# A fused mixer-and-experts block: its table of steps laid out with later landing times for two images

## The chip, the cores and the metric

The kernel runs on one core of one Trainium2 chip. The metric is the device time of one execution in microseconds (us); a change of about 1% is what a measurement of it can tell.

## What is computed

The input is 16 images of 64 channels by 16 x 16 pixels. Each image goes through a mixer with a depthwise convolution and a linear-attention product, and then each of its 256 tokens through a gated mixture of eight experts, of which two have weight:

```
x = x + conv_block(_ln_c(x))         # normalised over channels
  zxbcdt = x @ W_in.T                # z, (x, B, C), dt
  xBC = silu(depthwise 3x3 conv(xBC) + conv_b);  dt = softplus(dt + dt_bias)
  KV = einsum(B, xs * dA);  y = einsum(C, KV) + xs * D
  y = layernorm(y * silu(z)) * ln_g + ln_b;  out = y @ W_out.T
t = t + ffn(_ln_t(t))                # t: the tokens of x
  probs = softmax(xf @ gate_w + gate_b); cw = the top two of probs, else 0
  for e in 8 experts:  out += cw[:, e] * (gelu(xf @ W1[e] + b1[e]) @ W2[e] + b2[e])
```

## The kernel before

The 16 images are four groups of four (g = 0 to 3). A group is one pass of about 110 steps; a step has a short name and the group's number behind it, so `sq2` is the step "square the image" of group 2, the third. (Names such as `sq20` are the step `sq2` of group 0: the square behind the mixer. `x20` is likewise the step `x2` of group 0.) Groups share two sets of buffers by `g % 2`.

One list of tokens, `PLAN`, written out by hand as a table of text, sets the order of everything. Every engine walks the same list (`walk`) and emits the steps that have code in its own function, so each engine runs its steps strictly in the order of the list, and between engines only semaphores order the work. A step that waits therefore holds back all that stands behind it on its engine, and nothing on the others but what needs them.

The steps that matter here:

- Head of the kernel: `tb`, `tap` (VectorE) and `tw`, `tT` (TensorE) fold the depthwise taps into weight matrices; ScalarE's `tf` and VectorE's `te` copy them from PSUM to `wT`. `wa`, `wb` centre the experts' weights (`wae`, `wbe` copy them back). `busy` is a matmul on junk.
- Normalising group g: `sq` (ScalarE, L478) squares the image, `sm` (TensorE, L978) sums it, `se` copies the sums, `tr` transposes them, `ve` (VectorE) makes the variance, `pw` (GpSimd, L384) the reciprocal root, `rx` (ScalarE, L558) widens it, `rb` (TensorE, L991) transposes it back, `xn` (VectorE, L787) multiplies.
- Mixer: `cv0`, `cv1`, `cv2` (L1014, six matmuls a step, which the trace counts as twelve), `xs`, `z`, `sz`, `bd`, `bcp`, `k0` to `k2`, `bcs` (B and C's own convolution on VectorE), `dtv`, `ex`, `sf0`, `sf1` (softplus), `xt`, `v`, `bt`, `btc`, `kv`, `kvc`, `y`, `y0`, `y1`; then `gs`, `ps` (L1075), `stc`, `stt`, `gst`, `pwg`, `rxg`, `rbg`, `pj`, `pc`, `x2` for the second normalisation and the projection. `c0` and `cf` make a constant of the projection, `nm`, `nT` and `ne` prepare its weights.
- Experts: `sq2`, `s2`, `s2e`, `t2`, `ve2`, `pw2`, `rx2`, `rb2`, `xn2` normalise the tokens; `rt0`, `th`, `rt1`, `rt2` route them; `cwt` (L1107), `cwc` and the DMA step `gw` spread the eight weights to `gates` by way of DRAM. Expert e is `u` (up, L1124), `h` (gelu on ScalarE, L585), `d` (down, L1137), `m` (weigh on VectorE, L909), `a` (add on GpSimd, L419), each with the expert's number. Group 3 has PSUM banks of its own for this (its "lane"), the others share one set.

The image loads are not in `PLAN`. SyncE issues them ahead of it, those of groups 2 and 3 as the last of all:

```
            sp.dma_start(w2[:], W2.rearrange("e f c -> f e c")).then_inc(d_exp, 16)
            load(2)
            load(3)
```

ScalarE's square waits for its image by itself (`act.wait_ge(d_x[g], 32)`). Before a step whose function needs another table, ScalarE runs a one-element instruction, which loads the table (L440); the places follow from the order.

Of the kernel before, what the change touches and what calls it, by code (L numbers as in the profile page):

```python
# [15 lines left out]


PLAN = """
busy0 busy0 busy0 busy0 busy0 busy0 busy0 busy0 sq0 busy0 tb0 tw0 tap0 busy0 ta0 busy0 busy0 sm0 busy0 se0 busy0
tr0 tT0 ve0 ini0 sq1 sq2 pw0 wa0 te0 tf0 busy0 dtv0 rx0 sm1 wae0 rb0 wb0 se1 xn0 ex0 sf00 tr1 wbe0 cv00 sq3 ea0  # L20
ve1 nm0 pw1 bd0 cv10 bcp0 sf10 rx1 k00 cv20 k10 k20 nT0 xs00 rb1 xs10 z0 xn1 bcs0 xt00 dtv1 sz00 bd1 v00 sz10
xt10 ne0 bcp1 bt0 cv01 k01 v10 ex1 btc0 k11 kv0 cv11 kvc0 k21 sf01 bcs1 y0 sm2 cv21 se2 y00 gs00 y10 tr2 xs01
c00 ve2 gs10 xs11 sf11 ps0 pw2 cf0 xt01 stc0 stt0 z1 gst0 rx2 dtv2 rb2 pwg0 sz01 pj0 xn2 sz11 v01 xt11 rxg0 bd2
v11 pc0 rbg0 bcp2 bt1 x20 cv02 btc1 k02 sq20 s20 k12 kv1 s2e0 t20 cv12 ve20 ex2 kvc1 pw20 k22 y1 rx20 rt00 cv22
y01 th0 rb20 rt10 xs02 xs12 z2 xn20 gs01 rt20 u00 bcs2 sz02 y11 cwt0 xt02 cwc0 sz12 gw0 xt12 sf02 gs11 pj1 bt2
ps1 sf12 h00 pc1 u10 v02 stc1 btc2 stt1 v12 h10 d00 gst1 kv2 pwg1 u20 kvc2 y2 m00 rxg1 sm3 h20 y02 a00 d10 se3
rbg1 m10 gs02 tr3 u30 ve3 d20 x21 h30 pw3 u40 y12 sq21 a10 rx3 s21 rb3 m20 s2e1 gs12 t21 xn3 d30 a20 h40 ve21
bd3 dtv3 pw21 cv03 m30 bcp3 ex3 a30 rx21 rt01 rb21 cv13 k03 th1 xn21 rt11 u50 cv23 h50 k13 rt21 d40 xs03 k23
cwt1 xs13 z3 cwc1 ps2 gw1 m40 bcs3 sf03 a40 xt03 stc2 sz03 stt2 u60 sz13 xt13 gst2 d50 sf13 pwg2 pj2 h60 bt3 m50
rxg2 u70 v03 a50 btc3 pc2 rbg2 v13 x22 kv3 d60 kvc3 sq22 m60 y3 h70 s22 y03 s2e2 t22 u01 ve22 d70 y13 pw22 h01  # L30
gs03 u11 m70 a60 gs13 rt02 d01 h11 a70 pj3 m01 th2 u21 rx22 st0 rt12 a01 rb22 h21 d11 xn22 pc3 u31 rt22 m11 cwt2
cwc2 h31 ps3 gw2 a11 d21 stc3 stt3 u41 gst3 m21 pwg3 h41 d31 a21 u51 rxg3 m31 rbg3 h51 a31 d41 x23 u61 m41 sq23
h61 s23 a41 d51 s2e3 t23 m51 u71 ve23 d61 h71 pw23 m61 u02 a51 rx23 rt03 d71 h02 rb23 a61 m71 th3 u12 xn23 a71
rt13 u03 h12 st1 d02 h03 rt23 u22 m02 cwt3 u13 cwc3 h22 gw3 a02 d12 h13 u32 m12 d03 a12 h32 d22 u42 m22 u23 a22
h42 d32 h23 u52 m32 u33 a32 h52 m03 d42 a03 d13 m42 u62 a42 h33 m13 d23 a13 h62 u43 m23 d52 a23 h43 d33 m52 u53
a52 m33 d43 h53 a33 d62 m43 u63 a43 m62 d53 h63 u72 m53 u73 a53 h72 d63 a62 h73 d72 m63 a63 d73 m72 m73 a72 a73
st2 st3
""".split()


# [1128 lines left out]
```

## Time and profile before

| | us |
|---|---|
| median of 3 runs (lowest, highest) | 181.52 (181.01, 182.63) |
| the profiled execution | 181.16 |
| its span, first to last instruction | 179.3 |

| engine | busy us | share of span |
|---|---|---|
| TensorE (PE) | 152.0 | 85% |
| VectorE (DVE) | 121.2 | 68% |
| ScalarE (ACT) | 95.0 | 53% |
| GpSimd (POOL) | 64.5 | 36% |

The profile is of one execution. PE is TensorE's matmuls, PEld its weight loads, which overlap them. An idle time in brackets is followed by what ended it. The granted clock is 1.00 at TensorE's full speed.

### The profile page before, as it was taken

The numbers are of one execution on the slowest core, as the hardware profiler recorded it, in microseconds if no ns is written. First come the engines' busy times: TensorE is split into PE (matmuls) and PEld (weight loads), VectorE is DVE, ScalarE is ACT, GpSimd is POOL, SyncE is SP. The second block draws the span as 40 slices with busy tenths as digits, with TensorE's granted clock in tenths as the row PEclk, the third lists the DMA queues.
The fourth block names the chain that finished last, engine by engine and source line by source line (L and its number), as shares of the span: only waits on it lengthen the run. The fifth ranks groups of instructions, "written<-read, shape, count | busy, mean of one in ns | idle before, by whom it ended". The sixth has DMA issues, their size and how long they took to land.

```text
span 179.3 us, 2932 instructions
## 1 busy us (share of the span) xinstructions
PE 152.0 (85%) x966; PEld 61.2 (34%) x966; DVE 121.2 (68%) x330; ACT 95.0 (53%) x182; POOL 64.5 (36%) x83
## 2 busy tenths in 40 slices
PE   6930499999899999798899997895889699999960
PEld 2410334445444545343343443232232222223210
DVE  1640087899779899769999988995446973353461
ACT  1600524591662678746857674673474655855430
POOL 7430012000060300146530260652655623588580
PEclk9995589999999999999999999999999999999997
DMA  4604200000000000891000199020693025950004
GB/s 107 165 15 96 83 4 0 0 2 0 4 2 0 4 0 7 212 225 37 0 0 0 35 238 207 5 60 7 175 216 79 0 62 139 218 119 0 4 0 117
DMA packets 8344, 11.84 MB, mean 66 GB/s; under 512 B 3842, under 2 KB 7306, under 8 KB 7306
## 3 DMA queue, kind: packets, MB, share of 16 engines
q1 hardware_dynamic: 7152, 11.05, 26.9%
q10 hardware_dynamic: 1178, 0.61, 1.3%
q8 instruction: 8, 0.13, 0.3%
q14 instruction: 6, 0.05, 0.1%
HBM read 10.48 MB, written 1.18 MB: 65 GB/s over the span
## 4 chain that ended last, share of the span: by engine, by line
PE 63%; DVE 15%; issue 8%; DMA 5%; POOL 3%; ACT 3%; SPq 0%; DVEq 0%; POOLq 0%; ACTq 0%
PE pm L1014 14%; PE pe L1137 7%; PE pe L1124 6%; PE pe L1014 5%; PE pm L1137 4%; PE pm L1124 4%; DMA gates<-cwd 4%; PE pr L1141 3%; DVE tmp L909 3%; PE pm L1024 2%; PE pr L1075 2%; POOL acc L419 1%; DVE lg L671 1%; PE pm L1032 1%; PE pm L991 1%
## 5 line engine op out<-in xcount | busy, mean ns | idle before, releaser
L419 POOL TENSOR_TENSOR acc<-acc,tmp 128x512 f32<-128x512 f32 x27 | 34.3, 1276 | 26.1 <-DVE tmp L909 25.6
L585 ACT ACTIVATE hid<-pe,b1T 128x512 f32<-128x512 f32 x48 | 30.2, 681 | 12.5 <-PE pe L1124 12.3
L1124 PE MATMUL pe<-fst,w 64*128 64x512 f32 x96 | 26.9, 635 | 2.3 <-ACT hid L585 2.3
L909 DVE SCALAR_TENSOR_TENSOR tmp<-pe,b2T,gates 128x512 f32<-128x512 f32 x24 | 17.9, 746 | 13.9 <-PE pe L1137 12.6
L1137 PE MATMUL pe<-hid,w 128*64 128x512 f32 x96 | 25.8, 613 | 1.5 <-DVE tmp L909 1.5
L1014 PE MATMUL pm<-pad,wT 64*128 64x512 f32 x108 | 25.1, 600 | 0.0
L384 POOL TENSOR_TENSOR r<-ve,halves 128x8 f32<-128x8 f32 x4 | 6.6, 1662 | 40.9 <-DVE dtp L624 21.1
L612 DVE SCALAR_TENSOR_TENSOR bcc<-bcp,cw_bc,bcc 128x256 f32<-128x256 f32 x32 | 15.4, 482 | 1.0
L585 ACT ACTIVATE hid<-pm,b1T 128x512 f32<-128x512 f32 x16 | 10.1, 686 | 6.8 <-PE pm L1124 5.3
L1014 PEld LDWEIGHTS pm<-pad,wT 64*128 64x128 f32 x108 | 9.9, 185 | 11.0 <-issue 11.0
L402 POOL TENSOR_TENSOR rg<-ge,halves 128x8 f32<-128x8 f32 x4 | 6.6, 1642 | 18.5 <-DVE ge L863 18.5
L1124 PEld LDWEIGHTS pe<-fst,w 64*128 64x128 f32 x96 | 7.5, 184 | 15.4 <-issue 14.7
L409 POOL TENSOR_TENSOR r<-ve,halves 128x8 f32<-128x8 f32 x4 | 6.6, 1644 | 16.5 <-DVE ve L890 16.5
L440 ACT ACT_TABLE_LOAD x9 | 11.5, 1283 | 0.2
L909 DVE SCALAR_TENSOR_TENSOR tmp<-pm,b2T,gates 128x512 f32<-128x512 f32 x8 | 6.0, 750 | 7.4 <-PE pm L1137 6.7
L1124 PE MATMUL pm<-fst,w 64*128 64x512 f32 x32 | 8.7, 622 | 1.4 <-DVE fst L896 1.4
L1137 PEld LDWEIGHTS pe<-hid,w 128*64 128x64 f32 x96 | 5.1, 135 | 13.9 <-issue 9.5
L787 DVE TENSOR_TENSOR pad<-xin,pm 128x512 f32<-128x512 f32 x3 | 2.0, 683 | 10.9 <-PE pm L991 10.9
L978 PE MATMUL pe<-xin,sums 128*32 128x128 f32 x8 | 0.7, 417 | 9.7 <-issue 9.7
L1137 PE MATMUL pm<-hid,w 128*64 128x512 f32 x32 | 8.5, 609 | 0.2 <-DVE tmp L909 0.2
L1014 PE MATMUL pe<-pad,wT 64*128 64x512 f32 x36 | 8.5, 606 | 0.0
L478 ACT ACTIVATE sq<-xin 128x512 f32<-128x512 f32 x4 | 2.5, 624 | 10.5 <-DMA xin<-in_x_dram 10.4
(221 smaller groups left out, 249.6 us busy)
## 6 DMA issues: line engine op xcount, KB each, us to landing
gates<-cwd SPq DMA_DIRECT2D x16, 512.0 KB, 7.3
xin<-in_x_dram SPq DMA_DIRECT2D x7, 128.0 KB, 2.9
out_dram<-acc SPq DMA_DIRECT2D x7, 128.0 KB, 2.8
w<-in_L_ffn_W_dram SPq DMA_DIRECT2D x2, 256.0 KB, 3.4
w<-in_L_ffn_W_dram ACTq DMA_DIRECT2D x1, 256.0 KB, 4.4
xin<-in_x_dram ACTq DMA_DIRECT2D x1, 128.0 KB, 2.7
cwd<-cwS SPq DMA_DIRECT2D x4, 32.0 KB
out_dram<-acc ACTq DMA_DIRECT2D x1, 128.0 KB, 2.5
```

The source lines that it names most:

```text
L384: pool.tensor_tensor(r1[p][:], ve[p][:], halves[:], ALU.pow).then_inc(rstd.sem, 1)
L402: pool.tensor_tensor(rg[p][:], ge[p][:].rearrange("p j q -> p (j q)"), halves[:], ALU.pow).then_inc(o_rstd.sem, 1)
L409: pool.tensor_tensor(r2[p][:], ve2[p][:], halves[:], ALU.pow).then_inc(rstd2.sem, 1)
L419: pool.tensor_tensor(acc[p][:], (x2 if e == 0 else acc)[p][:], tmp[ln][e % 2][:], ALU.add).then_inc(summed[ln].sem, 1)
L440: act.activation(scrap[:, n:n + 1], zero[:], FUNCTION[step])
L585: act.activation(hid[ln][e % 2][:, q, :], expert_banks(g)[q][:], ACT.Gelu, bias=b1T[:, e:e + 1]).then_inc(hid_in[ln].sem, 1)
L612: dve.scalar_tensor_tensor(out=bcc[p][:], in0=view, scalar=cw_bc[:, t:t + 1], in1=bcc[p][:], op0=ALU.mult, op1=ALU.add).then_inc(bc_conv.s ...
L909: dve.scalar_tensor_tensor(out=tmp[ln][e % 2][:], in0=expert_banks(g)[2][:], scalar=b2T[:, e:e + 1], in1=gates[p][:, e, :], op0=ALU.add, o ...
L1014: ins = pe.matmul((b0, b1)[q][:], wT[half, t, :], pad[p][half, :, t // 3:t // 3 + HH, t % 3:t % 3 + WW], start=(t == 0), stop=(t == TAPS - 1))
L1124: ins = pe.matmul(expert_banks(g)[q][:], w1[half, e, :], fst[p][half, :], start=True, stop=True)
L1137: ins = pe.matmul(expert_banks(g)[2][C * q:C * q + C, :], w2[:, e, :], hid[ln][e % 2][:, q, :], start=True, stop=True)
L1141: pe.matmul(pr[1][:], junk[:, 0:P], junk[:], start=True, stop=True)
```

## The change

The table `PLAN` is written anew; no instruction's code is touched. All steps of before are in it, and one more `busy` (463 tokens for 461). The order on SyncE is the same; on the other four engines it is another. The head of the table:

```diff
-busy0 busy0 busy0 busy0 busy0 busy0 busy0 busy0 sq0 busy0 tb0 tw0 tap0 busy0 ta0 busy0 busy0 sm0 busy0 se0 busy0
-tr0 tT0 ve0 ini0 sq1 sq2 pw0 wa0 te0 tf0 busy0 dtv0 rx0 sm1 wae0 rb0 wb0 se1 xn0 ex0 sf00 tr1 wbe0 cv00 sq3 ea0
...
+busy0 busy0 busy0 busy0 busy0 busy0 busy0 busy0 sq0 busy0 tb0 busy0 tw0 tap0 busy0 ta0 busy0 busy0 sm0 busy0 se0
+busy0 tr0 tT0 ini0 ve0 pw0 wa0 tf0 te0 sq1 busy0 rx0 dtv0 sm1 rb0 ex0 se1 wb0 xn0 ea0 wae0 sf00 tr1 cv00 wbe0
...
```

ScalarE's order in the kernel's head, before; `sq0<-xin2` is the square of the third group's image, `sq1<-xin3` that of the fourth, `wT<-pe1` is `tf0`, `r1w0` is `rx0`:

```order
L478 ACTIVATE sq1<-xin1 128x512
L478 ACTIVATE sq0<-xin2 128x512
L452 ACTIVATE wT<-pe1 128x512
L558 ACTIVATE r1w0<-r10 128x512
L457 ACTIVATE w1<-pm2 128x512
L483 ACTIVATE s11<-pe0 128x256
L488 ACTIVATE dtu0<-dta0 128x64
L457 ACTIVATE w1<-pr0 128x512
L478 ACTIVATE sq1<-xin3 128x512
L461 ACTIVATE expA<-alog 128x8
```

The same place in the changed kernel:

```order
L452 ACTIVATE wT<-pe1 128x512
L478 ACTIVATE sq1<-xin1 128x512
L558 ACTIVATE r1w0<-r10 128x512
L488 ACTIVATE dtu0<-dta0 128x64
L483 ACTIVATE s11<-pe0 128x256
L461 ACTIVATE expA<-alog 128x8
L457 ACTIVATE w1<-pm2 128x512
L457 ACTIVATE w1<-pr0 128x512
```

The two squares are gone from here. They stand 14 to 15 rows further on, behind `btc0` (`bT0<-pm0`):

```order
L466 ACTIVATE woT<-pr0 128x64 x2
L467 ACTIVATE b1T<-pr0 128x8
L468 ACTIVATE b2T<-pr0 128x8
L515 ACTIVATE bT0<-pm0 128x8x16
L478 ACTIVATE sq0<-xin2 128x512
L478 ACTIVATE sq1<-xin3 128x512
L523 ACTIVATE gsq0<-g0 128x512
```

On TensorE, the stretch from the end of the first group's convolution (`xs0`, `bc0`, `v0` are group 0's) to the second group's first third (`pad1`), before:

```order
L991 MATMUL pe1<-ident,r1w1 128x128 x4
L1024 MATMUL pm2<-pad0,wT 128x512
L1024 MATMUL pm0<-pad0,wT 128x512
L1032 MATMUL pm1<-ident,xs0 128x128 x4
L1001 MATMUL pe2<-pad1,wbc 32x256 x4
L1032 MATMUL pm2<-ident,xs0 128x128 x4
L1038 MATMUL pm0<-ident,bc0 128x128 x2
```

and after:

```order
L991 MATMUL pe1<-ident,r1w1 128x128 x4
L1141 MATMUL pr1<-junk 128x512
L1024 MATMUL pm2<-pad0,wT 128x512
L1024 MATMUL pm0<-pad0,wT 128x512
L1032 MATMUL pm1<-ident,xs0 128x128 x4
L953 MATMUL pr0<-ident,wgc 128x64
L954 MATMUL pr0<-ident,wo_raw 128x64
L955 MATMUL pr0<-ident,b1_raw 128x8
L956 MATMUL pr0<-ident,b2_raw 128x8
L1032 MATMUL pm2<-ident,xs0 128x128 x4
L1038 MATMUL pm0<-ident,bc0 128x128 x2
L1001 MATMUL pe2<-pad1,wbc 32x256 x4
L1045 MATMUL pm0<-v0,bT0 32x128 x8
```

The projection's weights (`ident,wgc` and the three rows behind) now stand between the two transposes of `xs0`, the junk matmul is the added one, and `kv0` (`v0,bT0`) comes before the second group's convolution and not behind its first third.

Late in the kernel, on TensorE, around the first expert of group 3 (`pm0<-fst1,w1`) and the transpose `cwt3` (`ident,cw1`); `fst0` is group 2's input, before:

```order
L1102 MATMUL pr1<-ident,r2w1 128x128 x4
L1124 MATMUL pe0<-fst0,w1 128x512
L1124 MATMUL pe1<-fst0,w1 128x512
L1124 MATMUL pm0<-fst1,w1 128x512
L1124 MATMUL pm1<-fst1,w1 128x512
L1137 MATMUL pe2<-hid00,w2 64x512 x2
L1124 MATMUL pe0<-fst0,w1 128x512
L1124 MATMUL pe1<-fst0,w1 128x512
L1107 MATMUL pr1<-ident,cw1 64x128
```

and after:

```order
L1102 MATMUL pr1<-ident,r2w1 128x128 x4
L1124 MATMUL pe0<-fst0,w1 128x512
L1124 MATMUL pe1<-fst0,w1 128x512
L1137 MATMUL pe2<-hid01,w2 64x512 x2
L1124 MATMUL pm0<-fst1,w1 128x512
L1124 MATMUL pm1<-fst1,w1 128x512
L1124 MATMUL pe0<-fst0,w1 128x512
L1124 MATMUL pe1<-fst0,w1 128x512
L1107 MATMUL pr1<-ident,cw1 64x128
```

Group 3's first expert now stands behind one more down pass of group 2, and an up pass of group 2 and `cwt3` stand right behind it. In between these places, from the fourth group's mixer on, expert passes `u5` and `u6` of group 1 stand ahead of `cv03`, `bd3` behind it, `h6` behind `th1`, `kvc3` behind `rt02`, `xn22` behind `y03`, and `ps3`, `stt3` and `pj3` behind `cwt2` and `u51`.

## Rows read from the trace of the kernel before

**Rows 1.** The page, parts 1 and 5.
```profile
PE 152.0 (85%) x966; PEld 61.2 (34%) x966; DVE 121.2 (68%) x330; ACT 95.0 (53%) x182; POOL 64.5 (36%) x83
...
L585 ACT ACTIVATE hid<-pe,b1T 128x512 f32<-128x512 f32 x48 | 30.2, 681 | 12.5 <-PE pe L1124 12.3
...
L440 ACT ACT_TABLE_LOAD x9 | 11.5, 1283 | 0.2
```

**Rows 2.** Chain of waits in order of time: start us, us, what.
```profile
9.59 0.86 PE pm L947 x2
...
10.67 9.71 issue
20.38 1.08 PE pe L978 x16
21.46 1.05 PE pm L991 x4
22.50 1.56 PE pr L947 x2
...
24.28 2.78 PE pm L1014 x12
...
33.31 0.59 PE pe L991 x4
...
43.99 0.57 PE pm L978 x16
```

**Rows 3.** Timeline of ScalarE: start us, us, instruction [idle before, releaser].
```profile
8.15 0.63 ACT L478 ACTIVATE sq<-xin 128x512 f32<-128x512 f32 x1
19.16 0.63 ACT L478 ACTIVATE sq<-xin 128x512 f32<-128x512 f32 x1 [10.38 <-DMA xin<-in_x_dram]
...
20.18 0.62 ACT L558 ACTIVATE r1w<-r 128x512 f32<-128x512 f32 x1
```

**Rows 4.** Timelines of GpSimd and of VectorE, the first group's head.
```profile
9.53 1.66 POOL L384 TENSOR_TENSOR r<-ve,halves 128x8 f32<-128x8 f32 x1 [2.67 <-DVE ve L778]
...
22.64 0.69 DVE L787 TENSOR_TENSOR pad<-xin,pm 128x512 f32<-128x512 f32 x1 [10.60 <-PE pm L991]
```

**Rows 5.** Windows: us, then busy time of each engine, granted clock, DMA.
```profile
12.00:13.00 1.00, 0.00 (x0) 0.00 (x0) 0.04 (x1) 0.00 (x0) 0.00 (x0) 1.00 0.16 27
13.00:14.00 1.00, 0.00 (x0) 0.00 (x0) 0.00 (x0) 0.00 (x0) 0.00 (x0) 0.77 0.04 0
...
120.00:124.00 4.00, 2.02 (x17) 0.60 (x17) 3.46 (x14) 1.23 (x4) 0.74 (x2) 1.00 0.12 29
```

**Rows 6.** Timeline of SyncE, which issues the loads.
```profile
13.00 0.30 SPq L314 DMA_DIRECT2D b_raw<-in_L_ffn_b_dram  x1
...
15.56 2.58 SPq L294 DMA_DIRECT2D xin<-in_x_dram  x4
```

**Rows 7.** Timeline of TensorE, the second group's statistics.
```profile
48.63 0.65 PE L1075 MATMUL pr<-g,onesd 128*32 128x128 f32 x16 [0.56 <-ACT gsq L523]
```

**Rows 8.** What TensorE waited for, 78 to 174: total us, times, longest.
```profile
PE pr L1107 <- DVE cw L723: 1.7, 2, 1.5
...
PE pm L1124 <- DVE fst L896: 1.4, 1, 1.4
```

**Rows 9.** The window from 78 to 174, columns as in rows 5.
```profile
78.00:174.00 96.00, 87.22 (x501) 29.91 (x499) 67.85 (x167) 57.24 (x102) 48.41 (x37) 1.00 0.36 81
```

**Rows 10.** Timeline of VectorE: routing's first step, first and second group.
```profile
62.15 0.23 DVE L671 TENSOR_TENSOR lg<-t,r 128x64 f32<-128x64 f32 x1
...
90.04 1.28 DVE L671 TENSOR_TENSOR lg<-t,r 128x64 f32<-128x64 f32 x1
```

**Rows 11.** Timelines of ScalarE and VectorE: the fourth group's gates, a lone pass.
```profile
146.73 0.27 ACT L553 ACTIVATE cwS<-pr 64x128 f32<-64x128 f32 x1 [1.37 <-PE pr L1107]
...
156.02 0.75 DVE L909 SCALAR_TENSOR_TENSOR tmp<-pm,b2T,gates 128x512 f32<-128x512 f32 x1 [0.60 <-DMA gates<-cwd]
...
171.40 0.75 DVE L909 SCALAR_TENSOR_TENSOR tmp<-pm,b2T,gates 128x512 f32<-128x512 f32 x1 [2.17 <-PE pm L1137]
```

More of the change, by code:

```diff
@@ L18 @@
 PLAN = """
-busy0 busy0 busy0 busy0 busy0 busy0 busy0 busy0 sq0 busy0 tb0 tw0 tap0 busy0 ta0 busy0 busy0 sm0 busy0 se0 busy0
-tr0 tT0 ve0 ini0 sq1 sq2 pw0 wa0 te0 tf0 busy0 dtv0 rx0 sm1 wae0 rb0 wb0 se1 xn0 ex0 sf00 tr1 wbe0 cv00 sq3 ea0
-ve1 nm0 pw1 bd0 cv10 bcp0 sf10 rx1 k00 cv20 k10 k20 nT0 xs00 rb1 xs10 z0 xn1 bcs0 xt00 dtv1 sz00 bd1 v00 sz10
-xt10 ne0 bcp1 bt0 cv01 k01 v10 ex1 btc0 k11 kv0 cv11 kvc0 k21 sf01 bcs1 y0 sm2 cv21 se2 y00 gs00 y10 tr2 xs01
-c00 ve2 gs10 xs11 sf11 ps0 pw2 cf0 xt01 stc0 stt0 z1 gst0 rx2 dtv2 rb2 pwg0 sz01 pj0 xn2 sz11 v01 xt11 rxg0 bd2
@@ L24 @@
[L24 to L37, printed above, removed]
+busy0 busy0 busy0 busy0 busy0 busy0 busy0 busy0 sq0 busy0 tb0 busy0 tw0 tap0 busy0 ta0 busy0 busy0 sm0 busy0 se0
+busy0 tr0 tT0 ini0 ve0 pw0 wa0 tf0 te0 sq1 busy0 rx0 dtv0 sm1 rb0 ex0 se1 wb0 xn0 ea0 wae0 sf00 tr1 cv00 wbe0
@@ new lines @@
+ve1 sf10 pw1 bd0 cv10 bcp0 rx1 dtv1 k00 ex1 cv20 k10 k20 rb1 xs00 busy0 xs10 z0 nm0 bcs0 xt00 sz00 xn1 nT0 sz10
+v00 xt10 ne0 bt0 v10 bd1 btc0 sq2 kv0 bcp1 sf01 sq3 cv01 kvc0 k01 y0 sm2 y00 cv11 k11 gs00 se2 y10 tr2 cv21 ve2
+gs10 sf11 pw2 ps0 xs01 k21 xs11 z1 stc0 rx2 stt0 xt01 gst0 sz01 c00 rb2 v01 sz11 pwg0 xt11 cf0 xn2 bcs1 pj0 v11
+rxg0 bd2 dtv2 pc0 rbg0 bcp2 bt1 x20 cv02 btc1 k02 sq20 s20 k12 kv1 s2e0 t20 cv12 ve20 ex2 kvc1 pw20 k22 y1 rx20
+rt00 cv22 y01 th0 rt10 rb20 xs02 bcs2 z2 xn20 xs12 rt20 u00 sz02 sz12 y11 cwt0 bt2 cwc0 xt02 gs01 gw0 xt12 sf02
@@ new lines @@
+gs11 ps1 pj1 sf12 h00 btc2 u10 stc1 v02 v12 stt1 h10 d00 gst1 kv2 pc1 pwg1 u20 kvc2 y2 h20 m00 sm3 y02 a00 rxg1
+d10 rbg1 gs02 m10 u30 se3 x21 a10 tr3 h30 d20 ve3 sq21 u40 m20 pw3 y12 s21 h40 d30 a20 s2e1 dtv3 u50 rx3 m30 t21
+h50 rb3 ve21 d40 xn3 pw21 u60 m40 cv03 a30 rx21 rt01 gs12 a40 th1 h60 rt11 rb21 d50 xn21 pj2 rt21 ex3 u70 m50
+cwt1 bd3 cwc1 ps2 gw1 a50 bcp3 k03 d60 stc2 stt2 cv13 gst2 h70 k13 pwg2 pc2 m60 u01 rxg2 k23 a60 rbg2 h01 cv23
+sf03 bcs3 x22 d70 xs03 z3 m70 sq22 xs13 sf13 s22 a70 xt03 s2e2 sz03 t22 st0 d01 ve22 sz13 bt3 v03 pw22 xt13 btc3
@@ new lines @@
+m01 u11 v13 a01 rt02 h11 kv3 u21 kvc3 th2 rt12 d11 h21 y3 m11 rx22 u31 rt22 a11 rb22 h31 y03 d21 u41 xn22 gs03
+m21 cwt2 h41 y13 d31 a21 cwc2 gw2 u51 m31 gs13 ps3 a31 stc3 h51 stt3 pj3 gst3 d41 pwg3 pc3 u61 m41 rxg3 a41 h61
+rbg3 d51 x23 u71 m51 sq23 h71 s23 a51 d61 s2e3 t23 m61 u02 ve23 d71 h02 pw23 m71 u12 a61 rt03 rx23 d02 h12 rb23
+a71 m02 th3 u22 xn23 a02 st1 rt13 d12 h22 u03 rt23 u32 h03 m12 cwt3 cwc3 d03 h32 gw3 a12 d22 u13 m22 u42 a22 h13
+d32 h42 u23 m32 u52 a32 h23 d42 h52 u33 m42 u62 a42 m03 d13 a03 d52 h33 m13 a13 d23 h62 u43 m23 m52 u72 a23 h43
@@ L38 @@
+d33 a52 h72 u53 m33 a33 d62 h53 d43 m62 u63 a62 m43 d53 h63 a43 m53 u73 a53 d63 h73 d72 m63 d73 a63 m72 m73 a72
+a73 st2 st3
 """.split()
```

## The prediction

> **What bounds the kernel now.** I read the page first, then the chain of waits, then each engine's timeline around the holes of the chain. TensorE is busy 152.0 us, 85% of the span [rows 1]. The chain of waits runs along TensorE nearly everywhere, so the time is TensorE's work plus its holes plus the two ends. One hole dwarfs the others: 9.71 us from 10.67 to 20.38, put down to "issue" [rows 2]. What it really is stands in ScalarE's timeline: the square of the second group's image ends at 8.78, and the next instruction in ScalarE's order is the square of the third group's image, which waits 10.38 us for its transfer and starts at 19.16 [rows 3]. Behind it in the same queue stand `tf0`, the copy of the taps' transpose, and `rx0`, which widens the first group's reciprocal root into r1w and ran at 20.18 [rows 3]; TensorE needs them for `sm1` and `rb0`. The transfer was only issued at 15.56 or later, behind all small loads, the last of which were issued at 13.00 and after [rows 6]. So ScalarE waits in line for data that nobody needs yet. After the hole the order is dense: of the 96 us from 78 to 174 TensorE is busy 87.22 [rows 9], and waits are short [rows 8].
>
> **The change, part 1: sq2 and sq3 leave ScalarE's head.** They stand now behind `btc0`. The work is the same, so what counts is when the convolution of the first group (`cv00`) starts; it started at 24.28 [rows 2]. I walk the new head. The transposes of `tT` end as before, at 9.59, `wa0` at 10.45 and the filler at 10.67 [rows 2]. ScalarE does `tf0` as soon as the transposes are out (to about 9.95), then sq1 to about 10.55 (0.63 us [rows 3]). `sm1` then takes 0.57 us at full clock, as `sm2` does, against 1.08 in the hole's wake [rows 2]: 10.67 to 11.25. `rb0` needs `rx0`, which needs GpSimd's power, 9.53 plus 1.66, so 11.19 [rows 4], plus 0.62 for the widening [rows 3] and some 0.2 of hand-over: 12.05. It takes 0.59 instead of 1.05, `wb0` 0.86, as its twin `wa0` did at 9.59, instead of 1.56 [rows 2], and the two transposes of `tr1` 0.22. That gives 12.05 + 0.59 + 0.86 + 0.22 = 13.7 for `cv00`. Its input, `xn0`, is ready at 12.65 + 0.1 + 0.69 = 13.4 [rows 4], so it isn't late. Gain at this point: 24.28 - 13.72 = 10.55 us, of which 9.71 is the hole less a new one of 0.8, and 1.7 the half clock.
>
> What is late next? The biases' loads were issued before 13.0 [rows 6]. The convolution of B and C, their first user, follows `cv00` by some 5 us, so at about 18.7, and `nm0`, which reads the loads of 13.0 and was moved behind that convolution, comes at about 23.3. The third image had landed at 19.16 [rows 3]; the squares of the third and fourth are now due at 26.3. All have several us in hand, so I cost those waits at nothing; were the cover gone, each us late would be a us on the path.
>
> **Part 2: the new order up to 67 us.** `ex1` goes ahead of `xs00`, so two table loads go from ScalarE, beside which TensorE was working anyway: nothing. `kvc0` now stands behind the seven small steps of `sf01` on VectorE, but TensorE has `cv01` meanwhile, a third of a convolution, which takes 2.8 us as that of 24.28 did [rows 2]: nothing. `cv11` moves behind `sm2` and `c0` behind `ps0`, so that TensorE no longer waits 0.56 us for the square of g at 48.63 [rows 7]: gain 0.55. From `x20` to `th0` the two orders are the same, so the lead is 11.1 us and stays so; `u10` waits for `h00` in both. I place the end of `y2` at 66.9 (before 78.0). One junk matmul more (0.22 us) fills a stretch in which TensorE waits for `xs00` anyway.
>
> **Part 3: the rest, 78 to 174 us in the profile.** TensorE's holes are 96 - 87.22 = 8.8, less 0.6 after its last matmul, so 8.2 us [rows 9]. The largest are 1.5 before `cwt2`, which waits for the routing's last step on VectorE, and 1.4 before the fourth group's first expert (`u03`), which waits for `xn23` [rows 8]. In the new order `xn22` stands behind `y03`, and `cwt2` waits for it too; but `ps3` has been taken out from behind `cwt2`. `u03` stands later, behind `u22` and `d12`, when `xn23` is done: that 1.4 goes. Walked step by step with the durations of the trace, the new order's holes are about 0.35 before `d10`, 0.3 before `tr3`, 0.4 in small ones up to `kv3`, 0.7 before `u21`, 0.85 before `cwt2`, 0.45 before `d31`, and nine from 0.1 to 0.45 in the last 45 us, among them one for the fourth group's gates (0.45); sum about 6.3. The hole before `u21` shows how: ScalarE copies `btc3` until 100.4; `h11` then needs a table load (1.28) and its warm-up instruction (0.2), then two activations at 0.681 each less their overlap, 1.25 in all [rows 1], so it ends at 103.1, while TensorE's last step before, `kv3`, ended at 102.5; hand-over 0.1. That before `cwt2`: VectorE ends `rt22` at 108.4, `y03` and `xn22` (1.5 and 0.7) follow, so 110.65; TensorE ended `u41` at 109.8. Gain 1.9. Bounds: from both sides, no hole at all would gain 8.2; a rearrangement as poor as the worst stretch of before (120 to 124 us, where TensorE works 2.02 of 4 us [rows 5]), met twice more, would lose 2 to 4. I take 1.9, since short waits on neighbours are what the trace shows everywhere. What follows the last matmul (the last weighing, the last addition, the stores) is the same in both.
>
> My walk takes VectorE's small steps mostly at their lone price. The trace shows the dear one: the first of the routing takes 0.23 us alone and 1.28 us beside a GpSimd addition [rows 10]. The Trainium skill (page "SBUF — State Buffer", section "SBUF: two separate sides") has the rule: VectorE with two SBUF inputs and GpSimd lock one shared pair of ports for a whole instruction. The trace agrees with it. By that rule a denser schedule has more such meetings; at 1.05 us each by the rows, and about every second one on the path, two more would make 1 us. I leave it in the range.
>
> **Sum.** 10.55 + 0.55 + 1.9 = 13.0 us. The profiled execution took 181.16 us (span 179.3 and 1.86 around it), so 168.2; it lies 0.36 below the median of the runs, 181.52, so I forecast **168.5 us**.
>
> **The rivals.**
>
> *The later order gives some back* (chance 0.15). The experts' passes are pulled ahead (`u50`, `u60` before `cv03`), while `h60` waits behind `th1`, this behind `rt01`, this behind GpSimd's power `pw21` (1.65 us) and the power behind addition `a20`. If this chain and the one through `xn22` each cost 1.5 to 2 us instead of what I walked, the holes are 10 and not 6.3: 172 us. For it: part 3 of the order is new nearly throughout; against it: TensorE has three convolution steps of 2.8 us each to lay over these waits.
>
> *The clock falls in the new head as well* (0.07). The granted clock was still at full (2.4 GHz) in 12 to 13 us and fell to half (1.2 GHz) in the next us; TensorE had stood still since 10.67 [rows 2, 5]. It stayed full over waits of 1.5 us (120 to 124) [rows 5]. In the new head TensorE stands still for 0.8 us only, at 11.25 to 12.05. If it fell all the same, `sm1`, `rb0` and `wb0` would cost their 1.7 us again and the first convolution 1 to 2 more: 171 to 172 us. The Trainium skill (page "TensorE: Matmul & The Clock Gate", section "Part 4: PE-mode transpose") says that transposes don't count as busy the way matmuls do, and much of the head is transposes; by that rule this rival is the outcome. No row bears it out: the head's first transposes end at 9.59 [rows 2], and the clock was full in 12 to 13 [rows 5].
>
> *The later order fills nearly all holes* (0.1): at 2 to 4 us left, 164.5 to 166.5.
>
> *The hole isn't what I take it for* (0.04): a wait for several things is put down to the last, and another small load could be as late as the image. Then the gain is 0 to 8 us: 173 to 181. Against it: what stood behind the square ran without a further wait [rows 3].
>
> *Slower* (0.02). The fourth group's gates reach VectorE by DMA; from the copy at 146.73 to the first weighing at 156.02 it takes 9.3 us, ended by the DMA [rows 11]. They now land at about 143 us, while the third group still has passes that share TensorE with the fourth's. A pass that stands alone lasts 0.75 + 2.17 = 2.9 us from weighing to weighing [rows 11]. If the gates came only when the third group was done, at about 157, all eight passes of the fourth would stand alone: 8 x 2.9 = 23 us behind 157, then the end of 6, so a span of 186 and 188 us in all. It makes the kernel slower from about 7 us later than I place them.
>
> **Chances and range.** The forecast (166.5 to 170) has 0.62; the others as given. The range from 165.5 to 172.5 leaves out the end of the fullest order, the false hole and the slow case, about 0.15 in all. A measurement of this kernel tells about 1% from no change: faster by more than that (below 179.7) has 0.96, no change 0.02, slower 0.02.
>
> **What would show it.** In the changed kernel's profile ScalarE's third square should start at about 26 us without a DMA wait; `cv00` should start near 13.7 with the granted clock at full throughout; `y2` should end near 67; TensorE's holes from there to its last matmul (near 160) should add up to 6 or 7 us, with the largest before `cwt2` and `u21`; the span should be near 166. I am wrong if a new wait on a small load opens before 25 us, if the clock halves, or if the holes behind 67 us add up to 10 or more.

## The result, and the profile after

| | before | changed |
|---|---|---|
| median of 4 runs each, us | 181.86 | 173.53 |
| lowest to highest, us | 181.01 to 182.63 | 173.15 to 175.08 |
| profiled execution (its span), us | 181.16 (179.3) | 173.71 (171.8) |

The ratio is 0.9559, with a 95% interval of 0.9485 to 0.9634: the change makes the kernel 4.4% faster. I had forecast 168.5 us, with a range up to 172.5. The gain is 8 us where I had summed 13.

The page of the changed kernel, its busy times, granted clock and the chain's shares:

```profile
PE 151.1 (88%) x968; PEld 60.9 (35%) x968; DVE 123.9 (72%) x330; ACT 92.1 (54%) x178; POOL 64.9 (38%) x83
...
PEclk9999999999999999999999999999999999999995
...
PE 42%; DVE 28%; DMA 10%; issue 7%; POOL 6%; ACT 4%; SPq 1%; DVEq 0%; POOLq 0%; ACTq 0%
```

The chain's shares before:

```profile
PE 63%; DVE 15%; issue 8%; DMA 5%; POOL 3%; ACT 3%; SPq 0%; DVEq 0%; POOLq 0%; ACTq 0%
```

VectorE has done the same 330 instructions as before, in 2.7 us more [rows 1], and its share of the chain has nearly doubled. That is the first sign of what went wrong.

The head, on the chain of waits (start, length, what). It answers to [rows 2]:

```profile
9.75 0.18 DVE ve L778
...
10.01 1.67 POOL r L384
...
11.69 0.64 ACT r1w L558
...
12.37 0.66 PE pm L991 x4
13.03 0.86 PE pr L947 x2
13.89 0.22 PE pe L986 x2
14.11 2.78 PE pm L1014 x12
```

ScalarE's timeline (start, length, line, operation, in brackets the idle time before it), to be held against [rows 3]:

```profile
9.88 0.60 ACT L452 ACTIVATE wT<-pe 128x512 f32<-128x512 f32 x1 [1.40 <-PE pe L936]
10.37 0.62 ACT L478 ACTIVATE sq<-xin 128x512 f32<-128x512 f32 x1
11.69 0.63 ACT L558 ACTIVATE r1w<-r 128x512 f32<-128x512 f32 x1 [0.70 <-POOL r L384]
...
27.01 1.14 ACT L478 ACTIVATE sq<-xin 128x512 f32<-128x512 f32 x2
```

The 10 us hole is gone. The third image's square runs at 27.01 without a wait, and the convolution of the first group starts at 14.1 in place of 24.3. The clock is full up to the last of the 40 slices, which lies behind the last matmul.

The rest, by windows of the span (us, busy time and instructions of PE, PEld, DVE, ACT, POOL, clock), from the end of `y2` to the last matmul; it answers to [rows 9]:

```profile
68.20:166.00 97.80, 87.00 (x501) 30.34 (x499) 70.19 (x166) 57.24 (x102) 48.25 (x36) 1.00 0.36 79
```

TensorE's holes there are 97.80 - 87.00 = 10.8 us. They were 8.2 before, and I had walked 6.3. TensorE's waits, from 68 to 166 us, against [rows 8]:

```profile
PE pe L1137 <- DVE tmp L909: 2.1, 3, 0.9
PE pr L1107 <- DVE cw L723: 1.7, 2, 0.9
PE pr L1107 <- DVE fst L896: 1.3, 1, 1.3
PE pr L1091 <- ACT sq L538: 1.0, 2, 0.5
PE pe L1124 <- ACT hid L585: 0.8, 2, 0.4
PE pm L1137 <- DVE tmp L909: 0.8, 2, 0.6
PE pm L1045 <- DVE v L823: 0.7, 1, 0.7
```

Five of these seven rows, 6.6 us, end on VectorE. The longest, before `cwt2`, was 0.85 us in my walk and is 1.3. VectorE's and GpSimd's timelines ahead of it show why:

```profile
105.58 1.29 DVE L671 TENSOR_TENSOR lg<-t,r 128x64 f32<-128x64 f32 x1
...
111.01 1.04 DVE L717 TENSOR_TENSOR o<-k,kk 128x64 f32<-128x64 f32 x1
```
```profile
105.51 1.27 POOL L419 TENSOR_TENSOR acc<-x,tmp 128x512 f32<-128x512 f32 x1
110.66 1.31 POOL L419 TENSOR_TENSOR acc<-acc,tmp 128x512 f32<-128x512 f32 x1 [3.87 <-DVE tmp L909]
```

Two small steps that take 0.22 us alone take 1.29 and 1.04 here, and `xn22`, which `cwt2` waits for, stands behind both. Each ends 0.08 to 0.09 us after the addition that ran beside it: 105.58 + 1.29 = 106.87 against 105.51 + 1.27 = 106.78, and 112.05 against 111.97. They were held until the addition was over. In the order of before `L717` met none: 225 ns in the mean of its four, by the same grouping of before as the following rows. The groups of VectorE in the changed kernel by line (busy us, mean ns, idle time ahead):

```profile
L874 DVE SCALAR_TENSOR_TENSOR x<-xo,c,xin 128x512 f32<-128x512 f32 x4 | 3.5, 881 | 0.3
L795 DVE TENSOR_TENSOR dtv<-t,r 128x64 f32<-128x64 f32 x4 | 2.0, 490 | 0.9 <-POOL r L384 0.9
L717 DVE TENSOR_TENSOR o<-k,kk 128x64 f32<-128x64 f32 x4 | 1.7, 430 | 0.1
```

Before, their means were 752, 222 and 225 ns. Each has one step of four that met an addition and grew. A step with a single input, `L689` (`TENSOR_SCALAR td<-th`), was held too: at 136.12 it took 0.89 us, where it takes 0.18 alone, and ended at 137.01, behind an addition that ran to 136.95.

One correction to my text ahead of the result: the table has two junk matmuls more, not one (463 tokens against 461). One stands ahead of `tw0`, in the kernel's head; the other ahead of `z0`.

### The profile page after: what moved, and what is told of

Read it like the earlier page. It is cut to its first block, busy times and chain, and to the rows that moved or that the text cites. A ratio compares the mean times of both kernels' runs of the same rounds, so it can differ in the third digit from the quotient of the medians.

```text
span 171.8 us, 2932 instructions
## 1 busy us (share of the span) xinstructions
PE 151.1 (88%) x968; PEld 60.9 (35%) x968; DVE 123.9 (72%) x330; ACT 92.1 (54%) x178; POOL 64.9 (38%) x83
## 4 chain that ended last, share of the span: by engine, by line
PE 42%; DVE 28%; DMA 10%; issue 7%; POOL 6%; ACT 4%; SPq 1%; DVEq 0%; POOLq 0%; ACTq 0%
PE pm L1014 9%; DMA gates<-cwd 7%; PE pe L1014 5%; PE pr L1141 4%; PE pm L1137 4%; DVE tmp L909 3%; PE pm L1124 3%; DVE bcc L612 2%; DMA cwd<-cwS 2%; PE pe L1137 2%; DVE lg L671 2%; POOL r L409 2%; POOL r L384 2%; DVE g L849 1%; PE pm L1024 1%
## 5 line engine op out<-in xcount | busy, mean ns | idle before, releaser
L1124 PE MATMUL pe<-fst,w 64*128 64x512 f32 x96 | 26.3, 623 | 1.5 <-ACT hid L585 1.5
L612 DVE SCALAR_TENSOR_TENSOR bcc<-bcp,cw_bc,bcc 128x256 f32<-128x256 f32 x32 | 16.4, 511 | 1.0
L1014 PEld LDWEIGHTS pm<-pad,wT 64*128 64x128 f32 x108 | 9.9, 186 | 10.7 <-issue 10.2
L1124 PEld LDWEIGHTS pe<-fst,w 64*128 64x128 f32 x96 | 8.0, 185 | 14.1 <-issue 13.5
L523 ACT ACTIVATE gsq<-g 128x512 f32<-128x512 f32 x8 | 5.0, 626 | 12.8 <-DVE g L849 12.7
L1141 PE MATMUL pr<-junk 128*128 128x512 bf16 x17 | 7.2, 565 | 1.5 <-DVE zero L593 1.5
L849 DVE TENSOR_TENSOR g<-g,sz 128x512 f32<-128x512 f32 x8 | 6.6, 822 | 0.3
```

Source lines behind the costliest of these rows:

```text
L612: dve.scalar_tensor_tensor(out=bcc[p][:], in0=view, scalar=cw_bc[:, t:t + 1], in1=bcc[p][:], op0=ALU.mult, op1=ALU.add).then_inc(bc_conv.s ...
L849: dve.tensor_tensor(g_[p][:, q, :], g_[p][:, q, :], sz[p][:, q, :], ALU.mult).then_inc(g_dve.sem, 1)
L1014: ins = pe.matmul((b0, b1)[q][:], wT[half, t, :], pad[p][half, :, t // 3:t // 3 + HH, t % 3:t % 3 + WW], start=(t == 0), stop=(t == TAPS - 1))
L1124: ins = pe.matmul(expert_banks(g)[q][:], w1[half, e, :], fst[p][half, :], start=True, stop=True)
L1141: pe.matmul(pr[1][:], junk[:, 0:P], junk[:], start=True, stop=True)
```

## The experiments

Kernels are named by what they are; ratios are to the kernel before, run on the same chip. Differences between two of the kernels are those of their medians of four to six runs with a spread of 1 to 2 us, and some pairs ran on different chips, so a few tenths in them mean nothing. The head's start adds to this: in seven profiled executions that share the changed kernel's head, `cv00` starts anywhere from 12.81 to 14.04 us. Where a difference in the rest of the kernel matters, I therefore also give it from the end of `y2` on, from the profiled executions.

### Which part of the order costs: new head with the old rest, and the reverse

The table is cut right behind `y2` of group 2. The first kernel has the changed table up to there and before's behind it; against the changed table:

```diff
 ... kv2 pc1 pwg1 u20 kvc2 y2
-h20 m00 sm3 y02 a00 rxg1 d10 rbg1 gs02 m10 u30 se3
+m00 rxg1 sm3 h20 y02 a00 d10 se3 rbg1 m10 gs02 tr3
...
```

> The changed kernel's table up to step h20 (the end of y2 on TensorE), then the table of before. In the changed kernel TensorE reaches the end of y2 at 68.2 us, 9.9 us ahead of before, but its last matmul only 7.4 us ahead. Theory A, the new order of the later part is itself worse by 2.5 us: this kernel keeps the whole lead of 9.9 us, TensorE's holes behind y2 add up to 8.2 us as in before, span near 169.4 and time near 171.2 us. Theory B, whatever order follows loses the lead (later meetings of VectorE and GpSimd, or the gates' transfers, fall otherwise): the time is that of the changed kernel, 173.5 us.

Measured: 171.60 us (170.68 to 172.33), ratio 0.9423 (0.9336 to 0.9509). The second is the reverse cut: before's table up to `y2`, the changed one behind it.

> The table of before up to the same place, then the changed kernel's. Theory A: the hole on ScalarE's third square is back and the later part loses its 2.5 us as well, so slower than before by 2.5 us, near 184 us. Theory B: the later part of the new order is as good as the old one here, 181.5 us.

Measured: 186.01 us (184.70 to 186.15), ratio 1.0201 (1.0126 to 1.0276). The new rest makes the kernel slower with either head: by about 1.9 us on the new one (173.53 against 171.60; from the end of `y2` to the last matmul the profiled executions take 97.7 and 95.8) and by 4.2 on the old, where I had expected 2.5 (the spans of the profiled executions are 4.8 apart, 184.1 against 179.3). Of these 4.8, 3.1 lie in the rest: from the start of `z2` to that of the last matmul it takes 108.86 us where before takes 105.80. The others lie in the head, where the granted clock stayed at half longer than in before, which had it full from 24 to 28 us. The windows of the second kernel:

```profile
20.00:24.00 4.00, 3.00 (x22) 2.13 (x23) 0.74 (x2) 2.43 (x6) 0.00 (x0) 0.50 0.01 3
24.00:28.00 4.00, 4.00 (x13) 1.57 (x14) 3.17 (x14) 1.21 (x3) 1.18 (x1) 0.63 0.02 4
```

TensorE's waits from 60 us on in the first kernel (new head, old rest), the third and fourth row:

```profile
...
PE pr L1107 <- DVE cw L723: 1.7, 2, 1.5
PE pm L1124 <- DVE fst L896: 1.4, 1, 1.4
```

The wait for `xn23` of 1.4 is back, and yet the sum of the holes is 8.6 (96.00 - 87.40, from 67.9 to 163.9), 2.2 less than with the new rest.

### Is the hole what I took it for: the squares alone, and the loads alone

Before with only two tokens moved:

```diff
-... ini0 sq1 sq2 pw0 ... cv00 sq3 ea0 ...
+... ini0 sq1 pw0 ... cv00 ea0 ...
...
-... ex1 btc0 k11 ...
+... ex1 btc0 sq2 sq3 k11 ...
```

> The table of before with two tokens moved: sq2 and sq3 stand behind btc0, as in the changed kernel; nothing else. If the wait of the third square was the whole gain, cv00 starts near 13.5 us (one junk matmul less ahead of it than in the changed kernel), y2 ends at or before 68 us, and the time is 170.5 to 171.5 us by theory A and 173 us by theory B. If the rest of the new head order was needed (ex1 early, nm0 late behind the loads of 13 us), a new wait of VectorE on the loads in nm0 opens near 16 us and the time is 172 to 175 us.

Measured: 171.43 us (170.43 to 172.00), ratio 0.9411 (0.9339 to 0.9482). Two tokens give the whole of the change's gain, and 2 us more. `cv00` starts at 12.87. The new wait that the expectation named did open: VectorE waits 1.17 us for the biases' load in `nm0`, until 16.64, and TensorE has the convolution meanwhile.

The counter-test leaves the table of before as it is and only issues the third and fourth images' loads earlier:

```diff
             load(1)
+            load(2)
+            load(3)
             sp.dma_start(dtb[:], rows(dt_bias, P)).then_inc(d_dt, 16)
...
             sp.dma_start(w2[:], W2.rearrange("e f c -> f e c")).then_inc(d_exp, 16)
-            load(2)
-            load(3)
```

> The kernel before with its table of steps untouched: only the loads of the third and fourth images are issued right behind the second's, ahead of the small loads. If ScalarE's wait for the third image is the whole hole, sq2 can run at 11 to 12 us, a little late for tf0 and rx0, and cv00 starts at 14.5 to 16: a gain of 8 to 10 us, 172 to 174. If the hole was another, small load's, it is now issued some 2 us later and the time is 181 to 184. A new wait is possible at the small loads, for the biases ahead of the convolution of B and C (due near 19) or for A_log (13): up to 2 us more.

Measured: 171.57 us (171.14 to 172.76), ratio 0.9432 (0.9352 to 0.9512). The third square, still in its old place in ScalarE's order, waits 0.30 us in place of 10.38:

```profile
9.09 0.63 ACT L478 ACTIVATE sq<-xin 128x512 f32<-128x512 f32 x1 [0.30 <-DMA xin<-in_x_dram]
9.63 0.58 ACT L452 ACTIVATE wT<-pe 128x512 f32<-128x512 f32 x1
```

`cv00` starts at 13.67. One small load comes late, the biases' for `nm0` on VectorE:

```profile
17.69 0.28 DVE L757 TENSOR_TENSOR wg<-wo_raw,lng 64x128 f32<-64x128 f32 x1 [1.42 <-DMA b_raw<-in_L_ffn_b_dram]
```

It costs TensorE little: from the start of `cv00` to the end of `y2` this execution takes 54.5 us, and before 54.0. So the wait for the image was the whole hole, and there were two ways to remove it, neither of which needs a new rest. My expectation (172 to 174) had the square push `tf0` further back than it did: the image lands 2 us sooner than I had assumed.

### The added junk matmuls

```diff
-busy0 tb0 busy0 tw0 tap0
+busy0 tb0 tw0 tap0
...
-busy0 xs10 z0 nm0
+xs10 z0 nm0
```

> The changed kernel without the two junk matmuls that its table has more than before (the one ahead of tw0 and the one ahead of z0). By the traces the first moves tw0 from 5.41 to 5.83 us and so the whole head by 0.42; the second fills a wait. So 0.4 us less than the changed kernel, about 173.1 us. The rival: the head is bound by VectorE's tap products and not by the junk, then no difference.

Measured: 173.19 us (173.15 to 173.67), ratio 0.9519 (0.9458 to 0.9581). That is 0.34 less, as expected. In its profiled execution `cv00` starts at 12.82, 1.2 us sooner than in the changed kernel's (14.04 in the same view), but this can't be put down to the junk: the kernel with one fill for each addition, below, has both junk matmuls and the changed head, and its `cv00` starts as early:

```profile
12.81 2.85 PE L1017 MATMUL pm<-pad,wT 64*128 64x512 f32 x12
```

From the start of `cv00` to the end of `y2` it is 54.2 us with the junk and without it, so the second one filled a wait. The same edit on the new head with the old rest:

> The kernel with the new head and the old later order, without the two added junk matmuls. The changed kernel gained 0.34 us from their removal, so 171.2 us. Rival: the kernel with only the two squares moved ran its clock at half for 2 us behind a thin stretch of TensorE (2.02 of 4 us busy), which the kernel with the new head did not; 0.4 us earlier this one may fall to the same and take 172.5 us.

Measured: 170.75 us (170.21 to 171.48), ratio 0.9374 (0.9329 to 0.9418), 0.85 less than with the two, of which 0.4 was expected. This is faster than both kernels of the case.

### VectorE against GpSimd's additions

In the next two kernels 27 of GpSimd's 31 additions become one fill each, which reads nothing; all waits stay. The sum over the experts is left out in these and in the two with two fills below.

```diff
-                    pool.tensor_tensor(acc[p][:], (x2 if e == 0 else acc)[p][:], tmp[ln][e % 2][:],
-                                       ALU.add).then_inc(summed[ln].sem, 1)
+                    if e == 0:
+                        pool.tensor_tensor(acc[p][:], x2[p][:], tmp[ln][e % 2][:], ALU.add).then_inc(summed[ln].sem, 1)
+                    else:
+                        pool.memset(idle[p][:], 0.0).then_inc(summed[ln].sem, 1)
```

On the changed kernel:

> The changed kernel, where 27 of GpSimd's 31 additions of a weighed expert (all but each group's first) are replaced by a fill of a spare buffer of 128 x 950, about 0.95 us and without a read, so the experts' sum is left out. It has no two-input step of GpSimd for VectorE to meet except the first additions and the powers. Theory P (the ports): the later part lost its 2.5 us because VectorE's small steps met additions (1.28 us for 0.23 in the traces); then VectorE's busy time falls by 5 us or more and the kernel takes 170.5 to 171.5 us, level with the same edit on the kernel with the old later order. Theory O (the order): it lost them because steps that TensorE waits for stand behind others on VectorE; then it gains at most 1.5 us, and stays 2 us or more behind the other.

Measured: 166.93 us (166.55 to 167.15), ratio 0.9159 (0.9123 to 0.9195). On the new head with the old rest:

> The kernel with the new head and the old later order (171.6 us), with the same edit: 27 additions replaced by fills, the experts' sum left out. Theory P: it gains 0.5 us or less more than nothing, about 171, level with the edited changed kernel. Theory O: it gains as much as the changed kernel does, so 170 to 171 us, and stays 2 us or more ahead of it.

Measured: 166.64 us (165.99 to 167.26), ratio 0.9145 (0.9103 to 0.9187). The 1.9 us between the two rests shrink to 0.3, as theory P had it. But both theories missed the size by about 4 us: the additions cost the old rest nearly as much as the new one, where theory P gave them 0.5 us and theory O at most 1.5. The spare buffer `idle` has 950 columns here, and 800 in the control. The fill took 0.89 us and the addition 1.29, so this mixed two things. The control makes it long again, with two fills:

```diff
-                        pool.memset(idle[p][:], 0.0).then_inc(summed[ln].sem, 1)
+                        pool.memset(idle[p][:], 0.0)
+                        pool.memset(acc[p][:], 0.0).then_inc(summed[ln].sem, 1)
```

> The changed kernel with 27 of GpSimd's 31 additions of the experts replaced by two fills that read nothing: 128x800 into a spare buffer and 128x512 into the accumulator, by the rates of the single fill (0.89 us for 950 columns) 0.75 + 0.5 = 1.25 us in all, as long as the addition (1.29). The sum over the experts is left out, as in the runs with one fill. It parts the addition's length from its reading of SBUF, which the run with one short fill (166.93) mixed. If VectorE's meetings with the reading of the addition are the cost: as with the short fill, 166.5 to 168, VectorE busy near 116 us. If it is GpSimd's length, by which buffers come free and the gates' chain goes on: 172 to 174, VectorE's busy time still lower. In between: both, in proportion.

Measured: 167.25 us (166.72 to 168.48), ratio 0.9187 (0.9116 to 0.9258).

> The same two fills in the mixed order (new head, old order from 67 us on), the sum over the experts left out likewise. If only the reading costs: 166.5 to 167.5, and the two orders stay within 0.5 us of each other as with one short fill (166.93 and 166.64). If length counts: 170 to 171.6, and the two orders are about 2 us apart as with the additions.

Measured: 166.85 us (166.57 to 167.34), ratio 0.9158 (0.9103 to 0.9214). The length of GpSimd's step is worth 0.2 to 0.3 us at most, which these runs can hardly tell from nothing. By the medians its reading is worth 6.3 us in the changed kernel and 4.75 in the other. Part of that is the head's start, which no addition touches (the first runs behind `y2`): from the end of `y2` to the end of the span the profiled executions take 103.55 us with the additions and 98.19 with two fills in the changed kernel, 101.66 and 97.40 in the other. That makes the reading worth 5.4 and 4.3 us. The same place as above in the changed kernel with two fills (its lines are numbered 4 higher), VectorE, GpSimd and TensorE's `cwt2`:

```profile
108.01 0.23 DVE L721 TENSOR_TENSOR o<-k,kk 128x64 f32<-128x64 f32 x1
108.27 0.22 DVE L723 TENSOR_TENSOR o<-o 128x64 f32<-128x64 f32 x1
```
```profile
107.64 0.77 POOL L423 MEMSET idle<- 128x800 f32 x1 [3.85 <-DVE tmp L913]
108.34 0.52 POOL L424 MEMSET acc<- 128x512 f32 x1
```
```profile
110.96 0.27 PE L1111 MATMUL pr<-ident,cw 128*64 128x128 f32 x1
```

GpSimd runs beside the same small steps, and they take 0.23 and 0.22. The wait of 1.3 us before `cwt2` is gone. The step with a single input is another matter: the fills hold it as well, here until 82.21, behind a fill that ends at 82.16.

```profile
81.57 0.64 DVE L693 TENSOR_SCALAR td<-th 128x64 f32<-128x64 f32 x1
```
```profile
81.40 0.76 POOL L423 MEMSET idle<- 128x800 f32 x1
```

Behind `y2` the holes are 6.2 us:

```profile
68.00:160.40 92.40, 86.20 (x495) 29.82 (x486) 62.48 (x166) 56.70 (x101) 46.70 (x63) 1.00 0.38 84
```

### Two tokens back: is the order itself dearer?

The changed table with the weighing `m30` ahead of `dtv3` and `xn22` ahead of `y03`, so that what TensorE waits for comes first on VectorE:

```diff
-... s2e1 dtv3 u50 rx3 m30 t21 ... h31 y03 d21 u41 xn22 gs03
+... s2e1 m30 dtv3 u50 rx3 t21 ... h31 xn22 y03 d21 u41 gs03
```

> The changed kernel with two tokens of VectorE moved: m30 ahead of dtv3 (and not behind it), and xn22 ahead of y03. By theory O the two holes of TensorE that these steps end, 0.91 us before d40 and 1.30 us before cwt2, go, and no other opens: about 171.4 us. By theory P the moves change little, since the same small steps meet the same additions elsewhere: 173 us or more.

Measured: 172.59 us (172.37 to 175.00, 5 runs), ratio 0.9472 (0.9429 to 0.9514). That is 0.9 us less than the changed kernel, between the two theories, of which O had 2.1. The intervals of the two ratios overlap, so this is a sign and no proof. Its profiled execution is the slowest of the five by 2.1 us, so no row is read from it.

### Shorter additions, a try at a better kernel

The fastest order above, with each of the 31 additions (the expectation says 30) cut into two halves of the columns:

```diff
-                    pool.tensor_tensor(acc[p][:], (x2 if e == 0 else acc)[p][:], tmp[ln][e % 2][:],
-                                       ALU.add).then_inc(summed[ln].sem, 1)
+                    a, b = slice(0, HT // 2), slice(HT // 2, HT)
+                    src, t = (x2 if e == 0 else acc)[p], tmp[ln][e % 2]
+                    pool.tensor_tensor(acc[p][:, a], src[:, a], t[:, a], ALU.add)
+                    pool.tensor_tensor(acc[p][:, b], src[:, b], t[:, b], ALU.add).then_inc(summed[ln].sem, 1)
```

> The best kernel so far (mixed order without the two added junk matmuls, 170.75) with each of GpSimd's 30 additions split into two of half the columns (128x256 each); nothing else is changed and nothing left out. In the mixed order the reading of the additions cost 5 us in all. If a VectorE step that meets an addition waits for the end of that one instruction, the wait is at most 0.65 us in place of 1.27 and half as long in the mean: up to 2.5 us back, less some 0.1 us of fixed cost for each second half, of which little is on the path: 168.5 to 170. If the two engines share the SBUF's ports evenly while both run, the split changes nothing there: 170.7 to 171.5. If a VectorE step of two inputs of its own length meets both halves one after the other, or if GpSimd's fixed cost is larger than 0.1 us and its queue is what the powers wait behind, it is slower: up to 173.

Measured: 170.68 us (169.63 to 171.64, 6 runs), ratio 0.9327 (0.9267 to 0.9386), where the uncut one had 0.9374 (0.9329 to 0.9418): no difference that can be told, and less than the 0.75 to 2.25 us expected. From the end of `y2` to the last matmul the profiled executions take 94.6 us cut and 95.5 uncut, with 7.7 and 8.5 us of holes, but the cut one's `cv00` started 0.65 later (13.63 against 12.98). So a gain of under 1 us may hide here. VectorE's routing of group 2 beside the additions, uncut and then cut:

```profile
104.58 1.15 DVE L671 TENSOR_TENSOR lg<-t,r 128x64 f32<-128x64 f32 x1
105.76 0.23 DVE L676 TENSOR_TENSOR lg<-lg,gb 128x64 f32<-128x64 f32 x1
```
```profile
104.53 0.60 DVE L673 TENSOR_TENSOR lg<-t,r 128x64 f32<-128x64 f32 x1
105.17 0.65 DVE L678 TENSOR_TENSOR lg<-lg,gb 128x64 f32<-128x64 f32 x1
```

GpSimd in the cut kernel at that place:

```profile
104.33 0.73 POOL L421 TENSOR_TENSOR acc<-acc,tmp 128x256 f32<-128x256 f32 x1
105.01 0.73 POOL L422 TENSOR_TENSOR acc<-acc,tmp 128x256 f32<-128x256 f32 x1
```

One step is held to the end of the first half (104.33 + 0.73 = 105.06; it ends at 105.13), and the next to the end of the second (105.74; 105.82). The two together take 1.25 us, and took 1.38. The wait is per instruction, as expected, but a run of small steps meets both instructions. A half costs 0.73 and not half of 1.28, so GpSimd is busy 5.4 us longer (69.8 against 64.4); VectorE wins only 1.3 us (119.7 against 121.0).

## Why the prediction was wrong

The terms, each as forecast and as measured in the profiled executions:

| | forecast | measured |
|---|---|---|
| part 1, start of `cv00` | 10.55 | 24.28 - 14.1 = 10.2 |
| part 2, up to the end of `y2` | 0.55 | -0.2 |
| part 3, from there to the last matmul | 1.9 | -2.5 |
| sum | 13.0 | 7.4 |

The measured rows: `y2` ends at 68.2 (before 78.1) and the last matmul at 165.95 (before 173.38).

**The hole and its cause: right.** Moving the squares and moving the loads each take it away by itself. The rival that the hole might be another load's is refuted by the earlier loads, behind which all small loads came later and only one was waited for, 1.42 us on VectorE.

**Part 1 and 2: right in mechanism, 1.2 us too large in all.** In part 1, 0.4 us: I had the head start as before and missed the junk matmul ahead of `tw0`, which then starts at 5.83 and not at 5.41. As much lies within the scatter of the head's start, and that part 1 came within 0.4 is in part luck. In part 2, 0.8: I set `kv0`'s move at nothing, and TensorE waits 0.57 us before it, since `v10` runs on VectorE until 27.73. The other 0.2 stays open.

**Part 3: the step that failed.** It is the one in which my walk takes VectorE's small steps "mostly at their lone price", and puts the meetings with GpSimd's additions at "two more would make 1 us". Its holes, 6.3 us, were compared with the 8.2 of before, which are measured and have the meetings in them. The kernel with two fills is close to the one that I had walked: holes of 6.2 us, last matmul at 160.4 ("near 160"), 167.25 us. That the sum fits is in part luck, since single holes do not: `d10` waits 0.83 us in it where I had walked 0.35, and `cwt2` not at all where I had 0.85. With the additions reading, the same order has 10.8 us of holes and takes 173.53. So the meetings cost 5.4 to 6.3 us in the new order (by the rest alone, and by the medians). They cost 4.3 to 4.75 in the old rest with the same head, so of the 1.9 us by which the new rest is worse some 1.1 to 1.5 are meetings, and 0.4 to 0.8 is the order in itself. VectorE's busy time says the same: it falls by 8.0 us with the fills in the new order (123.9 to 115.9) and by 6.2 in the old rest (121.1 to 114.9); some two thirds to four fifths of each fall are on the path, where I had said every second meeting.

The rule of the Trainium skill that I cited and left "in the range" (page "SBUF — State Buffer", section "SBUF: two separate sides") describes it: a VectorE instruction with two SBUF inputs and a GpSimd one that reads SBUF exclude each other for a whole instruction. The runs agree: held steps end 0.07 to 0.09 us behind the addition, the routing's two-input steps beside a fill take their lone 0.22 to 0.23 us, and half as long an addition holds half as long. The step `td<-th`, which has one input and is held by additions and fills alike, is not covered by that sentence.

**The rivals.** "The later order gives some back" is the one that came, and 1.5 us beyond its 172; its chains through `th1` and `xn22` were only places of it. That the kernel with `xn22` and `m30` moved back is 0.9 us faster suggests that part of the loss can be had back by order alone, but does not show it. How this 0.9 divides between meetings avoided and a better order stays open. The clock did not fall in the new head. The fourth group's gates are another matter. I had placed them at about 143, and they end a wait of VectorE only at 149.36:

```profile
149.36 0.75 DVE L909 SCALAR_TENSOR_TENSOR tmp<-pm,b2T,gates 128x512 f32<-128x512 f32 x1 [0.76 <-DMA gates<-cwd]
```

That is 6.4 us late, close to the 7 from which I had called the kernel slower, and yet the wait is 0.76 us and the kernel 8 us faster. The whole rest was late as well, so this bound of mine does not hold.

What else stays open is what sets the head's start, and why an earlier one is worth less in the new order: without the junk `cv00` starts 1.2 us sooner there and the last matmul ends 0.4 sooner, and in the old rest it is 0.9 and 1.1.

## What to carry to other kernels

A walk with lone durations gives the time of a kernel in which no engine holds another; compare it with a walk of the old order by the same prices, never with the old order's measured holes. Where VectorE's two-input steps and GpSimd's SBUF-reading steps share a stretch, count the old profile's stretched steps first, and charge the new order at least as many, two thirds of them or more on the path, as here. And where a change mixes a fix of one large wait with a new order for everything, the fix alone (here two tokens, or one load issued earlier) may be the better kernel.

## What the runs showed of the hardware

The reading by GpSimd's additions cost more than I had thought: 5.4 to 6.3 us of 173.5, or 0.20 to 0.23 us for each of 27 additions. Cutting them finer helped by less than 1 us, if at all, as each piece holds a step of its own. A fill reads nothing, and the routing's two-input steps beside it took their lone 0.22 to 0.23 us, but it held the one-input `td<-th` for 0.64 us in place of 0.18.

The granted clock can fall late in the kernel behind a thin stretch. In the kernel with only the squares moved:

```profile
110.00:114.00 4.00, 2.02 (x37) 1.02 (x35) 2.81 (x13) 1.23 (x3) 0.94 (x1) 1.00 0.01 1
114.00:118.00 4.00, 4.00 (x21) 0.90 (x9) 1.29 (x5) 0.47 (x2) 0.82 (x2) 0.57 0.46 125
```

The same stretch in before has TensorE at work for 2.02 of 4 us as well [rows 5], with the same two holes of 1.47 and 0.51 us, and there the clock stayed full. So neither the busy share of such a stretch nor its holes tell whether it falls. From the start of `z2` to that of the last matmul this execution takes 107.75 us and before, whose order is the same there, 105.80; the kernel with the earlier loads, again of the same order, takes 106.06. So the fall costs some 1.8 us. The execution shown is the slowest of that kernel's four (172.00; the others 170.43 to 171.77).
